# Who moves the turned probability blocks: query tile 3 from ScalarE to VectorE, tile 2 left on ScalarE

## The reference, cut to what matters

```python
q  = concat(nq @ w_dq_nope, rope(nq @ w_dq_rope))          # 16 heads, 96 wide
k1 = concat(ckv @ w_dk_nope, rope(x @ w_krope / 16))       # latent keys
kw = x @ w_wink (its rope part rotated)                    # window keys
a1 = softmax(causal(q k1^T / sqrt(96))) @ v1               # 512 x 512 per head, causal
a3 = softmax(causal(q kw^T / sqrt(96))) @ vw               # the same
a2 = softmax(q ks^T / sqrt(96)) @ vs                       # 32 selected tokens
out = (gate[0]*a1 + gate[1]*a2 + gate[2]*a3) @ w_proj
x = x + ga * out
```

## Time and profile before

| | |
|---|---|
| median of 3 runs | 1849.78 us (1848.2 to 1859.12) |
| profiled execution | 1854.49 us, span 1852.7 us |
| mean granted TensorE clock | 0.961 |
| TensorE busy | 1715.3 us (93%) |
| ScalarE busy | 1220.4 us (66%) |
| VectorE busy | 1158.5 us (63%) |
| GpSimd busy | 680.2 us (37%) |
| turned copies | ScalarE 512 (L994, 277.4 us), VectorE 256 (L1463, 141.8 us) |

### The profile page before, as it was taken

One profiled execution on the slowest core, in us unless ns is written; L12 is line 12 of the kernel. 1 busy time (PEld: TensorE's weight loads), 2 busy tenths in 40 slices (PEclk: granted clock), 3 DMA queues, 4 the chain that ended last, 5 costly groups with the idle time before them and its releaser, 6 DMA issues.

```text
span 1852.7 us, 33815 instructions
## 1 busy us (share of the span) xinstructions
PE 1715.3 (93%) x10588; PEld 1067.9 (58%) x10588; DVE 1158.5 (63%) x3679; ACT 1220.4 (66%) x3383; POOL 680.2 (37%) x697
## 2 busy tenths in 40 slices
PE   5676689999999999999999999999999999999998
PEld 3433456665566656665666566665666566656664
DVE  5999666656555656655665656565565566565675
ACT  2564367766776757776676677675777677667773
POOL 0456533444333333434344433333333434443300
PEclk8787799999999999999999999999999999999999
DMA  4001021112111211212111211121122211121101
GB/s 171 1 0 28 17 64 41 41 37 64 27 43 36 51 44 41 52 45 52 41 41 36 64 29 43 38 50 42 41 52 45 52 41 41 40 62 30 42 19 46
DMA packets 71295, 80.91 MB, mean 44 GB/s; under 512 B 29520, under 2 KB 37840, under 8 KB 70992
## 3 DMA queue, kind: packets, MB, share of 16 engines
q1 hardware_dynamic: 71120, 78.76, 17.2%
HBM read 7.91 MB, written 2.10 MB: 5 GB/s over the span
## 4 chain that ended last, share of the span: by engine, by line
PE 72%; DVE 9%; ACT 8%; issue 6%; POOL 4%; DMA 0%; SPq 0%; DVEq 0%; POOLq 0%; ACTq 0%
PE bank L1862 24%; PE bank L1883 13%; PE bank L1826 8%; PE bank L1716 4%; PE bank L1717 3%; ACT arena L1002 2%; PE bank L1774 2%; PE bank L1789 2%; PE bank L1836 2%; DVE arena L1452 1%; PE bank L1712 1%; PE bank L1780 1%; PE bank L1783 1%; PE bank L1671 1%; PE bank L1770 1%
## 5 line engine op out<-in xcount | busy, mean ns | idle before, releaser
L1002 ACT ACTIVATE arena<-arena 128x512 f32<-128x512 f32 (+3 forms) x1024 | 571.4, 559 | 314.0 <-DVE arena L1452 309.2
L1452 DVE CUSTOM_DVE_ANT_0 arena<-bank,W 128x512 f32<-128x512 f32 (+3 forms) x1024 | 478.6, 487 | 464.9 <-PE bank L1862 436.7
L1862 PE MATMUL bank<-arena 96*128 96x512 f32 (+3 forms) x2048 | 698.8, 443 | 0.0
L1862 PEld LDWEIGHTS bank<-arena 96*128 96x128 f32 x2048 | 351.1, 192 | 192.6 <-issue 127.4
L1883 PE MATMUL bank<-W,arena 128*128 128x128 f32 x2560 | 420.1, 278 | 9.1 <-ACT arena L1002 7.1
L1883 PEld LDWEIGHTS bank<-W,arena 128*128 128x128 f32 x2560 | 309.6, 142 | 175.5 <-issue 103.7
L994 ACT ACTIVATE arena<-bank 128x512 f32<-128x512 f32 (+1 forms) x512 | 277.4, 542 | 126.4 <-PE bank L1883 121.6
L739 POOL TENSOR_TENSOR arena<-arena,one 128x512 f32<-128x512 f32 x64 | 66.5, 1040 | 722.3 <-DVE arena L1420 558.5
L1002 ACT ACTIVATION_READ_ACCUMULATOR arena<-arena 128x1 f32 x1024 | 195.9, 191 | 0.0
L1463 DVE COPY arena<-bank 128x384 f32<-128x384 f32 x256 | 141.8, 554 | 63.8 <-PE bank L1883 63.8
L1826 PE MATMUL bank<-arena 128*32 128x256 f32 (+1 forms) x3072 | 166.7, 350 | 0.0
(11 more groups left out here) (255 smaller groups left out, 2079.8 us busy)
## 6 DMA issues: line engine op xcount, KB each, us to landing
arena<-arena SPq DMA_DIRECT2D x896, 64.0 KB, 2.0
arena<-arena SPq DMA_DIRECT2D x64, 128.0 KB, 2.4
W<-wide SPq DMA_DIRECT2D x1, 3730.0 KB, 13.3
X<-x SPq DMA_DIRECT2D x8, 256.0 KB, 5.8
out<-arena SPq DMA_DIRECT2D x8, 256.0 KB, 2.3
arena<-arena SPq DMA_DIRECT2D x96, 16.0 KB, 1.8
LW<-lat SPq DMA_DIRECT2D x1, 768.5 KB, 14.3
arena<-mods SPq DMA_DIRECT2D x1, 768.0 KB, 4.7
```

The source lines that it names most:

```text
L1002: done = A(here, here, ACT.Exp, bias=nmax[:, c:c + 1], scale=-1.0, accum_out=lsum[:, c:c + 1])
L1452: last = v.tensor_tensor_reduce(Pb[:, s % 4, at_p:at_p + n], bank[turn.score_bank(s)][:, at:at + n], w("mask", T - n), -1.0, 3e38, ALU.add ...
L1862: last = MM(B_[:, at:at + n], query(t), Kb[a][g % 2][0:QD, h, 0:n], start=True, stop=True)
```

## The change

The copy of the turned blocks of query tile 3 (four blocks, 128x512) goes from ScalarE to VectorE. Tile 2 stays on ScalarE, tiles 1 and 0 on VectorE. The whole diff:

```diff
@@ -69,7 +69,7 @@
 PV_TALL, PV_LOW = 12, 15
 INVERT, SPREAD, MOVE, NORM, ADD = 12, 14, 15, 16, 17
-MOVER = {3: "act", 2: "act", 1: "dve"}
+MOVER = {3: "dve", 2: "act", 1: "dve"}
```

## The result

The changed kernel took 1870.16 us (median of 4 runs, 1865.0 to 1872.9), the kernel before 1848.99 us (4 runs, 1844.0 to 1859.1). The ratio is 1.0107, 95% interval 1.0087 to 1.0127, the difference of the medians +21.2 us. The forecast was 1866 us, +16. The profiled execution took 1872.92 us with a span of 1871.1 us, against 1854.49 and 1852.7 before.

A forecast was written before the change was run, and what follows sets the result against it. TensorE bounds the kernel, so only copies where the chain leaves it count: 9.8 + 4.6 - 2.1 + 0.9 + 1.4 + 2 = +16.6, less 0.6, gives +16 us on 1849.8, 1866 us; range 1846 to 1883.

The forecast's parts named there:

- What bounds the kernel, and the load: Whole kernel: TensorE busy 93%; a copy's own length gains or costs nothing, only places where the chain leaves TensorE count.
- The size of a copy: Each moved 128x512 copy on VectorE: 687 ns long, holding back the next operation by 0.61 us; VectorE busy 1334 us.
- Part 1, the turning stall: Groups 1 and 3, second half: unit 14's copy delays VectorE's string before TensorE's transposes, 16 x 0.61 = +9.8 us.
- Part 2, the merge stall: First half of groups 0, 1, 2: L1435's wait for GpSimd swallows unit 2's copy; 0.2 us left 23 times, +4.6 us.
- rival (a): At L1435 and L1265: copies are not swallowed and these end late, +31 to +36 us, 1881 to 1886; chance 0.20.
- Part 3: Remaining places: group 3 -2.1, group 0 +0.9, group 2 +1.4, first and last groups about +1 us each.
- (b): At the new VectorE copies: they contend with GpSimd themselves, waiting some 0.6 us each, +50 us; chance 0.03.
- (c): At the turning step too, VectorE's idle time takes the copies up, hiding them: 1850 +- 4 us; chance 0.10.
- (d): At the merges: ScalarE's relief shortens the waits, up to 0.58 us in each of 23 places, 1834 us; chance 0.07.

The follow-up runs named there:

- E8: Kernel before with L1398 written at step 15, not 16, and copies of units 0, 4, 6, 16, 18 on VectorE: 1840.71 us, ratio 0.9963.
- B: The changed kernel run again, all eight tile 3 units copied by VectorE, against the kernel before: 1865.33 us against 1850.08, ratio 1.0088.
- E2: Kernel before with only unit 14 of tile 3 copied by VectorE: 1863.06 us, ratio 1.0062.
- E3: Kernel before with all tile 3 units except unit 14 copied by VectorE: 1856.69 us, ratio 1.0045.
- E5: Kernel before with only unit 2 of tile 3 copied by VectorE: 1860.81 us against 1849.16, ratio 1.0053.
- E6: Kernel before with unit 2 copied by VectorE, plus an extra VectorE copy of the same size ahead of it that nobody reads: 1874.8 us, ratio 1.0140.
- E9: Kernel before with units 0, 4, 6, 12, 16, 18 copied by VectorE, units 2 and 14 left on ScalarE: 1860.62 us against 1849.42, ratio 1.0057.
- E4: Kernel before, no moved copies, with L1398 written at step 15 in place of 16: 1838.5 us against 1850.08, ratio 0.9939.
- E10: Kernel before with L1398 at step 15 and only units 12 and 14 of tile 3 copied by VectorE: 1853.97 us against 1849.42, ratio 1.0009.

## Why the prediction was right, point by point

**What bounds the kernel, and the load.** Right. E8 shows it: 160 copies changed engine and the time stayed. Two copies of the eight carry the loss, because of what stands behind them.

**The size of a copy** was right in its length (0.687 us) and in its step (0.60 to 0.62 us in the rows above). The forecast of busy time was not: I counted 256 x 0.687 and got 1334 us, but busy time counts overlapping instructions once, so that each adds 0.61, and the waits that L1435 and L1265 lost come off. 1158.5 + 256 x 0.61 = 1314.7, less 24 x 0.60 for L1435, makes 1300 and was measured as 1296.0. In the same way ScalarE gave back not 0.596 but 0.46 us a copy, 118 us and not 153.

**Part 1, the turning stall, +9.8 us.** Right: +0.60 us in each of the second halves of groups 1 and 3, in B and in E2, in no kernel of the old order that leaves unit 14 on ScalarE (E3, E5, E6, E9), and nothing in group 0. E2 gave +12.2 us at equal clock. Of the 2.4 us above 9.8, 1.2 are the second half of group 2, longer by 0.17 us seven times; the rest is not settled.

**Part 2, the merge stall, +4.6 us.** Right in mechanism: L1435 went from 1.31 to 0.71 us and ended where it had, the residue was 0.21, 0.23 and 0.12 us at the merges of groups 1, 2 and 0 (0.2 forecast for each), with E5 at +4.8 us, and E6 shows that a second copy is not swallowed. So rival (a) was 0.16 us away (L1435 now starts that long before L703 ends), and it is what E6 built.

**Part 3.** Mixed, and its errors cancelled. Group 3's first half gained 0.05 us and not 0.3 (the 1.80 us of L1435 is there), group 2's second half lost 0.14 (forecast 0.2), and in the second half of group 0 the clean value went from 18.92 to 18.75 us, a gain of 0.17 where I had a loss of 0.13. A turn at full clock, added up from the shortest values of its nine stretches, lengthened by 1.66 us, forecast 1.7 (198.42 to 200.08). By groups that is 0.81, 0.37, 0.54 and -0.05 us in groups 1, 2, 3 and 0, where the forecast had 0.8, 0.4, 0.3 and 0.2: the forecast was too low for group 3 and too high for group 0 by about the same 0.25. Over seven turns the 1.66 are 11.6 us. All that stands ahead of the first L1351, the first group with it, took 2.9 us more (457.26 and 460.20 us), where the forecast had 1 for the first group. The granted clock was the same there (0.99 in both from 235 us on), so it isn't the clock; units 12 and 14 stand ahead of a maximum there, but no run shows how much is theirs. The last part, from L1308 of its group 0 to the last L1308, took 133.93 us against 131.32, +2.6, as the forecast had it (two turning stalls, two merges' residues and +1 for the last group). 11.6 + 2.9 + 2.6 = 17.1 us, against +15.3 and +16.0.

**The rivals.** (b), contention of the copies themselves: out, the longest of 512 copies at L1463 took 693 ns. (c), hidden, fell with the turning stall; it describes only the six units of E9. (d), faster, fell with the merges: no kernel of the old order has one that is more than 0.08 us shorter than before. **What I had not priced** is the clock. My 4.7 us between the profiled execution and the median was taken over as a constant; by the fitted line it is the clock (0.961 against the 0.965 that the kernel before has in the median of the experiments' runs, and 4 x 1.48 = 5.9 us). A change of structure can move it, as E5 and E9 show with +7 and +11 us that no wait explains (the move is measured; that the structure causes it is an inference from its being in all six executions of E9). That it hardly moved for B (0.964) is the part of the hit that was luck; the first set of runs, at 1870, had it lower (0.960 in the profiled execution).

**Open.** At equal clock E2 and E3 sum to 19.7 us and B has 16.0, while their fixed stretches sum to 14.2 and 13.2. The 3.7 us are more than the fit's uncertainty. Either the parts overlap outside the turns, in the first and last groups, or the straight line for the clock is too simple. And what decides in which turns the clock falls was not tested.

## What to carry to other kernels

Cost a moved instruction by what stands behind it in its new queue, not by the load of the two engines: of eight copies of the same length one cost 12 us, one 5, and the six others together nothing at equal clock (E9). Where the next instruction is itself waiting for another engine's lock or result, a copy ahead of it is nearly free until the margin is used up, and then costs its whole length; and an instruction that isn't needed at once (L1398) is worth moving out of such a string, which alone gave 0.6% here (E4, 1838.5 us, the fastest). Before believing a difference under 1%, cut the trace into stretches that repeat and look at the granted clock of those that don't.

## What the runs showed of the hardware that was not expected

- **The clock falls at two fixed places of a turn, in some turns only.** In the kernel before, windows of 2 us around the one in group 0 show what TensorE did before and after (columns as above; the column ahead of the DMA share is the granted clock):

```profile
660.00:662.00 2.00, 1.27 (x6) 0.69 (x6) 1.96 (x8) 0.77 (x2) 0.00 (x0) 1.00 0.48 114
662.00:664.00 2.00, 0.96 (x5) 0.73 (x5) 1.97 (x4) 0.05 (x1) 1.82 (x3) 0.69 0.43 103
664.00:666.00 2.00, 2.00 (x8) 1.37 (x6) 1.78 (x6) 1.73 (x4) 1.14 (x4) 0.50 0.42 99
...
670.00:672.00 2.00, 2.00 (x9) 1.00 (x8) 0.00 (x0) 1.09 (x2) 0.00 (x0) 1.00 0.02 2
```

  TensorE has waits (1.27 and 0.96 us busy of 2.00), then works without a gap at 0.50, which is 1.2 GHz, and some 6 us later at 2.4 GHz again. In group 3 the same order of events stands at 1180 us (1.44 us busy of 2.00 at 0.90, then 0.50, 0.75 and 1.00). At full clock the 48 instructions of the first place take 8.73 us, and 11.35 with the fall. In E3 and E9 it strikes every second turn of the six (18.76 and 21.38 us in turn in E9), in E10's second half of group 0 never. By the fitted slope E9's median is some 12 us higher through its lower clock, in both places together (0.9565 against 0.965; an estimate).
- **A VectorE sum of two SBUF inputs and GpSimd's sums exclude each other in the order in which they come.** L1435 took 0.69 to 0.71, 0.90, 1.31 or 1.80 us for the same 128x512 sum, by where in GpSimd's string it began; begun 0.01 us after L701 it waited for the whole of it and ended 0.55 us after its end. When it was L1435 that came first, by 0.30 us, GpSimd's L701 took 1.73 us and not 1.26. The copies from PSUM at L1463 were never held so: the longest of 512 took 693 ns. The Trainium skill, page "SBUF — State Buffer", section "Who interferes with whom", describes this as a lock for the whole instruction, first come first served, and these lengths agree with it.
- **Busy time given back is less than the durations.** A 128x512 copy lasts 596 ns on ScalarE, but taking one away shortened ScalarE's busy time by 0.46 us on average, since neighbours overlap.
